# Turning the quantised activation tile of a linear layer by a transposing DMA instead of by TensorE products

## What is computed

```
x = x + attention(layernorm(x))          # 32 query heads of 16, 8 key/value heads of 16, plus a memory term
x_q = round_to_float8(clip(layernorm(x) / s, -448, 448)) * s     # s is input_scale, bfloat16
x = x + x_q @ (weight * weight_scale).T  # weight is 512 x 512 in float8
```

## Time and profile before

| | |
|---|---|
| device time, median of 3 runs (lowest to highest) | 2101.21 us (2100.49 to 2101.35) |
| device time of the profiled execution | 2100.72 us |
| its span, first to last instruction | 2099.0 us |
| mean granted TensorE clock | 0.994 of full speed |
| PE busy | 97% of the span |
| ACT busy | 93% |
| DVE busy | 55% |
| DMA, mean over the span | 61 GB/s |

### The profile page before, as it was taken

How to read it: one execution, slowest core, us unless ns; L and a number is a source line. 1 busy time by engine, 2 the same in 40 slices (tenths; PEclk the granted TensorE clock), 3 DMA queues, 4 the chain that set the end, 5 groups by cost and what they waited for, 6 DMA issues and landing times.

```text
span 2099.0 us, 63902 instructions
## 1 busy us (share of the span) xinstructions
PE 2045.4 (97%) x27826; PEld 883.7 (42%) x27826; DVE 1148.8 (55%) x1768; ACT 1942.9 (93%) x2180; POOL 83.6 (4%) x135
## 2 busy tenths in 40 slices
PE   7999799999999999999999999999999999999996
PEld 4555343344444444444343444444434444444442
DVE  5666554445555545555455555455554455554556
ACT  4444699999999999999999999999999999999995
POOL 3222000000000000000000000000000000000000
PEclk9999999999999999999999999999999999999998
DMA  5554411111111211121111211111112111121111
GB/s 188 177 176 137 123 47 47 47 42 33 47 48 47 67 30 40 47 67 47 47 33 42 67 47 47 41 51 45 48 47 67 35 40 47 47 67 47 30 40 41
DMA packets 119739, 127.96 MB, mean 61 GB/s; under 512 B 13696, under 2 KB 96000, under 8 KB 119488
## 3 DMA queue, kind: packets, MB, share of 16 engines
q1 hardware_dynamic: 117424, 121.42, 20.4%
q10 hardware_dynamic: 2064, 2.69, 0.4%
HBM read 86.57 MB, written 37.49 MB: 59 GB/s over the span
## 4 chain that ended last, share of the span: by engine, by line
PE 92%; DVE 3%; SPq 2%; ACT 1%; issue 1%; DMA 0%; ACTq 0%; POOL 0%; DVEq 0%
PE ps L722 42%; PE ps L744 42%; PE ps L673 3%; PE ps L789 1%; PE ps L775 1%; PE ps L687 1%; DVE pool L887 1%; SPq L339 1%; SPq L327 1%; PE ps L649 1%; DVE parts L912 0%; DVE norm L916 0%; DVE y_out L994 0%; DMA mem_aug<-in_memory_norm 0%; PE ps L767 0%
## 5 line engine op out<-in xcount | busy, mean ns | idle before, releaser
L623 ACT ACTIVATE pool<-ps 128x1024 f32<-128x1024 f32 x1984 | 1833.9, 1133 | 17.9 <-PE ps L722 13.1
L722 PE MATMUL ps<-q_st,k_st 99*32 99x512 bf16 x16384 | 1105.2, 379 | 10.0 <-DMA v_st<-v_aug 9.9
L744 PE MATMUL ps<-pool,v_st 128*32 128x512 f32 (+1 forms) x8704 | 1077.1, 567 | 0.3 <-ACT pool L623 0.3
L722 PEld LDWEIGHTS ps<-q_st,k_st 99*32 99x32 bf16 x16384 | 445.0, 96 | 801.9 <-issue 412.4
L744 PEld LDWEIGHTS ps<-pool,v_st 128*32 128x32 f32 x8704 | 276.4, 111 | 211.5 <-ACT pool L623 1.2
L1076 DVE SCALAR_TENSOR_TENSOR parts<-parts 128x1024 f32<-128x1024 f32 x192 | 235.2, 1225 | 6.6
L1083 DVE STREAM_TRANSPOSE by_token<-ps 128x512 f32<-128x512 f32 x64 | 45.9, 717 | 290.6 <-PE ps L744 290.6
L1062 DVE TENSOR_SCALAR parts<-ps 128x512 f32<-128x512 f32 x128 | 88.6, 692 | 132.4 <-PE ps L722 132.4
L1138 DVE SCALAR_TENSOR_TENSOR y_out<-ps,scalars,resid 128x512 f32 x28 | 21.0, 751 | 216.4 <-PE ps L775 216.4
L673 PE MATMUL ps<-pool,wqT 128*128 128x512 f32 x256 | 113.9, 592 | 0.0
L578 ACT ACTIVATE parts<-ps 128x512 bf16<-128x512 f32 x40 | 23.9, 597 | 75.7 <-PE ps L673 75.7
(11 more groups left out here) (123 smaller groups left out, 823.2 us busy)
## 6 DMA issues: line engine op xcount, KB each, us to landing
q_st<-q_aug SPq DMA_DIRECT2D x384, 64.0 KB
v_st<-v_aug SPq DMA_DIRECT2D x64, 256.0 KB
q_aug<-parts SPq DMA_DIRECT2D x96, 128.0 KB
k_st<-k_aug SPq DMA_DIRECT2D x64, 192.0 KB
sigma_kept<-y_out SPq DMA_DIRECT2D x32, 256.0 KB, 3.2
k_st<-k_aug SPq DMA_DIRECT2D x64, 128.0 KB
wqT<-sigma_kept SPq DMA_DIRECT2D x32, 256.0 KB, 3.2
resid<-in_x SPq DMA_DIRECT2D x7, 1024.0 KB, 8.0
```

What stands on the lines that cost most here:

```text
L623: act.activation(held[:, half_u * 2 * CH:half_u * 2 * CH + 2 * CH], sc[unit % SLOTS].rearrange("p a b -> p (a b)"), ACT.Exp, scale=EXP_UNIT)\
L722: last = pe.matmul(dst[VW * c:VW * c + VW, :], k_st[0:AUG, par, keys:keys + VW], q_st[0:AUG, par, q * CH:q * CH + CH], start=True, stop=True)
L744: last = pe.matmul(acc[par][VW * c:VW * c + VW, :].rearrange("v (i s) -> v i s", s=VW)[:, places, :], v_st[:, par, j, :], by_place[:, c, p ...
```

## The change

For the 28 tiles in trips 4 to 31, SP now issues four DMAs with `transpose=True` from `xq_now` to `xqT`, each a block of 128 x 128 bfloat16 (32 KB), after the loads of the odd head. They wait for `xq_ready`, and for the previous tile's result. `ffn_turn` and `take_turned` go away. PE's quarter products move from u = 23, 25, 27, 29 to u = 10, 14, 18, 22 of the odd head. The first waits for all four DMAs and for DVE's reading of the late scores, which lie in the bank that the product writes. DVE waits for the previous tile's four DMAs before it writes `xq_now`.

```diff
-FFN_TURN_AT = 21
-FFN_PRODUCT_AT = (23, 25, 27, 29)
+FFN_PRODUCT_AT = (10, 14, 18, 22)
...
+            sp.sem_inc(xqT_loaded, SIXTEEN_FREE)
...
+            def turn_tile(tile):
+                sp.wait_ge(xq_ready, tile + 1)
+                sp.wait_ge(y_ready, tile + ONE_FREE)
+                sp.sem_inc(turn_begun, 1)
+                for k in range(KT):
+                    sp.dma_start(xqT[:, k, :], xq_now[:, k * P:k * P + P], transpose=True).then_inc(xqT_loaded, 16)
+
             for h in range(HEADS):
                 load_block(1, h)
+                if h % 2 == 1:
+                    turn_tile(h // 2)
             with sp.Fori(2, NG) as g:
                 for h in range(HEADS):
                     if h == 2:
                         store_chunk(g - 2)
                     load_block(g, h)
+                    if h % 2 == 1:
+                        turn_tile((g - 1) * TPC + h // 2)
...
-            def ffn_turn(tile, n):
-                pe.wait_ge(late_taken, n * LATE + LATE)
-                pe.wait_ge(xq_ready, tile + 1)
-                pe.wait_ge(y_ready, tile + ONE_FREE)
-                for k in range(KT):
-                    for c in range(P // VW):
-                        features = k * P + c * VW
-                        last = pe.matmul(ffn_turned[VW * c:VW * c + VW, k, :], xq_now[:, features:features + VW],
-                                         ident_bf[:, :], start=True, stop=True)
-                last.then_inc(xq_turned, 1)
-
-            def ffn_product(tile, k):
+            def ffn_product(tile, n, k):
                 if k == 0:
-                    pe.wait_ge(xqT_ready, tile + 1)
+                    pe.wait_ge(late_taken, n * LATE + LATE)
+                    pe.wait_ge(xqT_loaded, (tile + 1) * 16 * KT + SIXTEEN_FREE)
...
-                        if u == FFN_TURN_AT:
-                            ffn_turn(ffn, n)
                         if u in FFN_PRODUCT_AT:
-                            ffn_product(ffn, FFN_PRODUCT_AT.index(u))
+                            ffn_product(ffn, n, FFN_PRODUCT_AT.index(u))
...
                 dve.wait_ge(f_step, i * FLOAT8_STEPS + 6)
+                dve.wait_ge(xqT_loaded, i * 16 * KT + SIXTEEN_FREE)
                 dve.tensor_tensor(xq_now[:, :], xs, big, ALU.subtract).then_inc(xq_ready, 1)
-
-            def take_turned(g, t):
-                dve.wait_ge(xq_turned, g * TPC + t + 1)
-                dve.tensor_copy(xqT[:, :, :].rearrange("p k s -> p (k s)"), ffn_ps).then_inc(xqT_ready, 1)
...
-                    take_turned(g - 1, hp)
                     ffn_out(g - 1, hp)
```

More of the change, by code:

```diff
@@ L43 @@
 ONE_FREE, TWO_FREE, THREE_FREE = 1, 2, 3
+SIXTEEN_FREE = 16
 LATE = 2
@@ L195, in attention_ffn @@
         weight_tp = acc[0][:, 0:CH // 2].bitcast(BF16)
-        ffn_turned = acc[0].rearrange("p (k s) -> p k s", k=KT)
         last_ffn_tp = [ps[:, i, 0:CH // 2].bitcast(BF16) for i in range(2)]
@@ L280, in attention_ffn @@
         xq_turned = sem("xq_turned")
+        turn_begun = sem("turn_begun")
+        xqT_loaded = sem("xqT_loaded")
         xqT_ready = sem("xqT_ready")
@@ L626, in _ @@
             for t in range(TPC):
-                act.wait_ge(xq_turned, (NG - 1) * TPC + t + 1)
+                act.wait_ge(xq_turned, t + 1)
                 act.activation(last_xqT[:, t, :, :].rearrange("p k s -> p (k s)"), last_ffn_tp[t % 2], ACT.Copy)\
@@ L846, in last_ffn_turn @@
                 if t >= 2:
-                    pe.wait_ge(xqT_ready, (NG - 1) * TPC + t - 1)
+                    pe.wait_ge(xqT_ready, t - 1)
                 for k in range(KT):
@@ L852, in last_ffn_product @@
             def last_ffn_product(t):
-                pe.wait_ge(xqT_ready, (NG - 1) * TPC + t + 1)
+                pe.wait_ge(xqT_ready, t + 1)
                 for k in range(KT):
```

## The result

| | before | after |
|---|---|---|
| median of 5 runs, us | 2100.49 (2100.31 to 2101.35) | 2089.96 (2089.18 to 2090.80) |
| profiled execution, us | 2100.72 | 2089.18 |
| its span, us | 2099.0 | 2087.5 |

The ratio is 0.9948 (95% interval 0.9937 to 0.996), so the changed kernel is about 0.5% faster, 10.5 us by the medians and 11.5 us between the profiled executions. Forecast were 2088.0 us, in a range of 2085.0 to 2096.5.

What follows compares the result with a forecast made beforehand. PE was taken as the bound, with 57.24 us of its own work in a 57.52 us trip. The turn's 6.1 us and the products' 7.1 us made 13.2 us off 2100.72, so a median of 2088.0 us, range 2085 to 2096.5.

Steps and rivals of the forecast that it cites:

- The bound: Over one trip PE's own work, 57.24 of 57.52 us, sets the pace; ACT needs 56.05 us.
- The turn, 0.22 us a trip, 6.1 us: Odd head: the turn leaves PE, freeing 0.22 us in each of 28 trips, 6.1 us in all.
- backlog: Claim that PE is the late engine at the turn in the odd head, so the freed 0.22 us counts.
- The move of the products, 7.1 us: Odd head: products at u = 10, 14, 18, 22 remove PE's 0.285 us wait, less 0.03, 28 times: 7.1 us.
- The wait that remains, 0.03 us: Next even head: PE enters with about 0.15 us more lead; its cost was taken as 0.03 us per trip.
- The DMAs are hidden: Transposing DMAs, odd head: landing some 6 us after `xq_now`, before the product at u = 10, so they cost nothing.
- the margin of 8 us: Time left between the DMAs' landing, some 6 us after `xq_now`, and the first product, 14.1 us after it.
- the forecast's three granularities: Packet sizes per tile: 2 bytes (239 us), 32 bytes (14.9 us) or 256-byte rows (1.9 us), the last taken.
- The rule on one descriptor per element: Skill page's rule for non-contiguous last dimensions; would hold if DMAs move element by element, about 8,500 us, chance 0.04.
- The slower rival's price: DMAs late at PE's u = 10, odd head: 2197 us (32-byte pieces, chance 0.08) or about 8,500 us (chance 0.04).
- Each us costs 28 us: Each us of DMA landing later than 14.1 us after `xq_now` costs 28 us, once per each of 28 trips.
- The sum: Whole kernel: 6.1 + 7.1 = 13.2 us off the profiled 2100.72 us, giving 2087.5 us; median 2088.0 us.

Runs made afterwards that it cites:

- Two placements: Changed kernel with products moved to u = 11, 16, 21, 26 (2088.29 us, again 2087.58) or to 12, 17, 22, 27 (2088.24 us).
- other places: Kernel before with PE's own turn moved to u = 14 and products to 20, 23, 26, 29: 2094.34 us, ratio 0.9968.
- The second run of the changed kernel: The change measured again, unaltered, against the kernel before: 2088.89 us, ratio 0.9941.

## Why the prediction was right, and where its terms were off

- **The bound.** Right. PE sets the pace, and its own work of 57.24 us less the turn's 0.22 is the floor of a trip. Two placements stand on it, in three traces (57.02 and 57.03), and no kernel is below.
- **The turn, 0.22 us a trip, 6.1 us, "an engine that has a backlog at that point".** The size of the work was right, and "backlog" was half wrong. PE came to the turn from a stretch in which it waited for ACT. Taken alone, the turn gave 0.12 us per trip, because a fourth wait opened in its place. Where the places leave no wait it gives all of it: 57.26 us with PE's turn at 14, 57.02 or 57.03 with the DMA and products at 11, 16, 21, 26.
- **The move of the products, 7.1 us.** Larger when it comes on top of the turn: 57.38 less 57.08 us per trip, 0.30 x 28 = 8.4 us. With PE's turn kept, other places gave 0.24. The parts alone make 0.12 + 0.24 = 0.36 of the 0.43 us: they help each other, since the wait that the one opens the other fills. The forecast's two terms hold where both changes are made, and neither can be had at its price alone.
- **The wait that remains, 0.03 us.** It measured 0.06 and came at unit 22 of the even head, not in units 0 to 5, where I had looked for it by the earlier trace rows. As a price this is 0.8 us of the whole.
- **The DMAs are hidden.** Right. Some 6 us from `xq_now` to the landing were forecast, and 7.1 us it was (716.18 to 723.3). The composition was off: an issue takes 1.23 us and not 0.36, and most of the time is issue, while a small packet took some 20 ns and not 58. The two errors partly cancel, so that the forecast came near is luck; the margin of 8 us would have carried either. Of the forecast's three granularities 256-byte rows is the one that the 160 packets fit. By the Trainium skill ("Advanced Engine Details and Errata", X-Bar Transpose) these DMAs are as fast as regular ones; here the landing was 2.3 against 1.8 us, and SP's issue twice as long, so the trace agrees for the data (1.1 against 1.2 us behind the issue) and not for the queue. The page's bandwidth no run here shows. The rule on one descriptor per element ("DMA: Bandwidth & Descriptors", Rules for kernel authors) didn't apply: 160 packets per DMA.
- **The slower rival's price.** "Each us costs 28 us" was too low. Beyond that point a trip lost 5.5 us for 3.4 us of waiting, and PE came back at half clock each time.
- **The sum.** 13.2 us were forecast and 11.5 measured between the profiled executions. Per trip it is right: 57.52 less 0.475 is 57.05, and 57.08 was found, 12.3 us for 28. Of the other 0.8 us, 0.4 are lost ahead of the first tile. The second stage starts with PE at half clock, after it has waited for loads, and how long that lasts differs from run to run. From 238 to 240 us, before and then after (PE busy, clock, DMA share, GB/s):

```profile
238.00:240.00 2.00, 2.00 (x36) 1.00 0.33 98
```

```profile
238.00:240.00 2.00, 2.00 (x20) 0.64 0.30 88
```

16 matmuls fewer in these 2 us are about 0.9 us of time. At the start of the first trip with a tile 0.4 us of it are left: the same scores begin at 467.79 us before and at 468.17 after. Another 0.2 us go at the end: after the last head PE's last weighing waits 0.48 us for ACT, and 0.26 in the kernel before. Nothing in the change touches the start of the second stage. The second run of the changed kernel came out at 12.3 us under its own runs of before, so I take the start as scatter, but no run settles it.

## What to carry to other kernels

Where two engines are coupled by a few buffers and both are nearly full, count over one period what each needs, and look for the stretch where the bounding engine waits for the other. Work taken out can be lost in such a wait, and fixed work moved into it is gained: here the places alone gave 0.24 us of a trip, and the removed turn alone 0.12. Spread side work evenly over the period, its last piece included. A DMA that replaces engine work is free only up to its first consumer; measure the margin by issuing it twice, and three times, since beyond it the price was 1.6 times the wait.

## What the runs showed of the hardware that was not expected

- A transposing DMA of a 128 x 128 bfloat16 block, SBUF to SBUF, holds SP's queue for 1.23 us (median of 112), and its plain copy for 0.60 us. It makes 160 packets, the plain copy 144. A load from device memory of twice the size holds the queue for 0.37 us (median of 384 in the kernel before), and for 0.71 us in the trip of the earlier trace rows (4.28 us for six).
- The copy and the transposing form left the kernel with the same stretch, 1512.5 us, and so did eight DMAs in place of four.
- A small packet of these DMAs took some 20 ns of an engine's time (an estimate from the queue's share before and after), where the mean packet of the queue took 58.
- After a wait of 4.3 us TensorE was granted 0.50 of its clock for about 5 us, though it was fully busy again from the first moment.
